# A graph layer on one core: a tile's routed rows are scattered one group later, and both adds of a pair stand together

## What is computed

```python
xn = layernorm(x)
# 1. a mean over each node's incoming edges, and a linear attention over all nodes
mean = segment_sum(xn[src], dst) / max(count, 1)
g  = relu(relu(mean @ Wl.T + bl + xn @ Wr.T) @ Wln.T + xn)
kv = einsum(k, v) / 6250              # per head, k and v normalised
m  = gelu((q @ kv + xn) @ w1 + b1) @ w2 + b2 + xn
x  = x + g + m
# 2. a mixture of experts: one shared, and for each row the best 2 of 8
xf = layernorm(x)
shared = gelu(xf @ W1s + b1s) @ W2s + b2s          # 256 -> 1024 -> 256
routed = sum over the row's 2 experts of weight * (gelu(xf @ W1p[e] + b1p[e]) @ W2p[e] + b2p[e])
out = x + shared + routed
```

## Time and profile before

| | |
|---|---|
| median of 3 runs | 3546.64 us (3541.11 to 3561.95) |
| the profiled execution | 3547.38 us, span 3545.6 us, TensorE clock 0.859 |
| TensorE, weight loads, VectorE, ScalarE, GpSimd busy | 71%, 60%, 30%, 24%, 52% |
| gathers at L508 | 1568, 995 ns each |
| scatters at L530 | 98, 1002 ns each |
| adds at L539 | 78, 1616 ns each |
| chain that ended last | TensorE 5% of the span, DMA 1% |

### The profile page before, as it was taken

One profiled execution on the slowest core, in us unless ns is written; L12 is line 12 of the kernel. 1 busy time (PEld: TensorE's weight loads), 2 busy tenths in 40 slices (PEclk: granted clock), 3 DMA queues, 4 the chain that ended last, 5 costly groups with the idle time before them and its releaser, 6 DMA issues. The chain is left out here.

```text
span 3545.6 us, 52520 instructions
## 1 busy us (share of the span) xinstructions
PE 2515.2 (71%) x12336; PEld 2115.0 (60%) x12337; DVE 1072.2 (30%) x3518; ACT 861.9 (24%) x1897; POOL 1843.6 (52%) x1790
## 2 busy tenths in 40 slices
PE   0687765655667677776868777768687787878698
PEld 0455554554556566665657666657576676666598
DVE  8344421222222223232323232223232332324221
ACT  1233211121212122221212222212122222223243
POOL 2666555545455655555455655555556556552121
PEclk9889877777779889888889898879898988989799
DMA  7333232222233343434343434343434344342564
GB/s 223 94 87 89 82 87 79 79 74 82 67 121 111 109 122 109 129 103 129 101 130 109 136 111 131 103 122 106 131 109 138 110 133 135 110 136 68 156 199 128
DMA packets 256257, 405.93 MB, mean 114 GB/s; under 512 B 70074, under 2 KB 187002, under 8 KB 255579
## 3 DMA queue, kind: packets, MB, share of 16 engines
q0 software_dynamic: 95360, 232.54, 24.2%
q1 hardware_dynamic: 154218, 164.36, 14.7%
q10 hardware_dynamic: 6384, 6.42, 0.5%
HBM read 362.16 MB, written 41.01 MB: 114 GB/s over the span
## 5 line engine op out<-in xcount | busy, mean ns | idle before, releaser
L508 POOL DMA_INDIRECT region<-xn_d,idx_s x1568 | 1560.5, 995 | 744.1 <-issue 470.8
L1380 PE MATMUL p_agg<-region,onehot 128*128 128x258 f32 x3136 | 751.5, 395 | 24.7 <-issue 15.1
L1601 PE MATMUL p_y<-region 128*128 128x256 f32 x1248 | 385.4, 444 | 438.7 <-ACT region L664 360.7
L1380 PEld LDWEIGHTS p_agg<-region,onehot 128*128 128x128 f32 x3136 | 608.4, 198 | 135.4 <-issue 43.0
L1601 PEld LDWEIGHTS p_y<-region 128*128 128x128 f32 x1248 | 270.8, 223 | 505.6 <-ACT region L664 379.3
L530 POOL DMA_INDIRECT slot_d<-xfp_s,posi_s x98 | 98.1, 1002 | 603.0 <-DVE xfp_s L1159 587.7
L664 ACT ACTIVATE region<-p_h,b_h 128x256 f32<-128x256 f32 x312 | 144.4, 473 | 921.4 <-remote 624.0
L854 DVE TENSOR_TENSOR late<-late,p_agg 128x258 f32 x176 | 74.6, 424 | 842.9 <-remote 532.8
L1590 PE MATMUL p_h<-wkv_s,region 128*128 128x256 f32 x1248 | 319.6, 384 | 9.7 <-ACT wkv_s L657 5.0
L1566 PE MATMUL p_y<-w2s_s,work 128*128 128x256 f32 x784 | 255.4, 408 | 97.5 <-ACT work L671 57.5
L848 DVE TENSOR_TENSOR onehot<-row_s,iota_s 128x896 f32<-128x896 f32 (+1 forms) x225 | 245.9, 1093 | 235.4 <-issue 232.3
(11 more groups left out here) (255 smaller groups left out, 2885.9 us busy)
## 6 DMA issues: line engine op xcount, KB each, us to landing
region<-in_w1p SPq DMA_DIRECT2D x55, 1024.0 KB
region<-in_w2p SPq DMA_DIRECT2D x55, 1024.0 KB
region<-xn_d,idx_s POOLq DMA_INDIRECT x1568
rows_s<-slot_d SPq DMA_DIRECT2D x39, 258.0 KB
region<-in_x SPq DMA_DIRECT2D x7, 896.0 KB, 5.1
xn_d<-region ACTq DMA_DIRECT2D x7, 896.0 KB, 6.5
rows<-in_x SPq DMA_DIRECT2D x49, 128.0 KB
xnr_s<-xn_d SPq DMA_DIRECT2D x49, 128.0 KB
```

What stands on the lines that cost most here:

```text
L508: pool.indirect_dma_start(out=ring[b][:, u, 0:D], out_offset=None, in_=xn_d, in_offset=IND(ap=idx_s[b][:, u:u + 1], axis=0)).then_inc(s_ro ...
L1380: m = mm(p_agg[b % 2], onehot[:, b % 2, u, :], ring[b][:, u, :], start=u == 0, stop=u == U - 1)
L1601: m = mm(p_y[:, h, :], hid2_s[:, j, h * P:(h + 1) * P], w2p_s[0][:, j, :], start=j == 0 and h == 0, stop=j == KF - 1, skip_group_check=True)
```

## The change

GpSimd's order in a step becomes: gathers of group 0, `scatter_slots`; gathers of group 1, `add_pair(0)`, `add_pair(1)`; gathers of group 2; gathers of group 3. The scatter is no longer that of the payload just being written but of the one before: a new register `paid` counts the payloads scattered (it starts at 2, the value of `pay` after the first payload), and a step scatters only if `paid` is behind `turn`. So a payload written at the end of one of TensorE's steps is scattered behind the first group's gathers of GpSimd's next iteration; an iteration without a tile does it at the same place. After the loop two scatters are left where there was one. Both adds of a pair follow the gathers of group 1. The number of DMAs of each kind is the same.

```diff
             def next_edges(edges):
                 word.look_up(edges[0] + 1)
-                plain(edges)
+                for b in range(RING):
+                    gather_edges(b)
+                    if b == 0:
+                        with pool.If_lt(paid, turn):
+                            scatter_slots()
+                pool.reg_add(turn16, turn16, 16)

             def scatter_slots():

                 pool.wait_ge(S["const"], 3)
-                pool.wait_ge(S["pay"], turn)
+                pool.wait_ge(S["pay"], paid)
                 for k in range(TOPK):
                     pool.indirect_dma_start(out=slot_d, out_offset=IND(ap=posi_s[:, k:k + 1], axis=0),
                                             in_=xfp_s[:, k, :], in_offset=None).then_inc(S["sc"], 16)
+                pool.reg_add(paid, paid, 1)
...
                 for b in range(RING):
                     if edges is not None:
                         gather_edges(b)
+                    if b == 0 and second:
+                        with pool.If_lt(paid, turn):
+                            scatter_slots()
                     if b == 1 and second:
                         with pool.If_lt(unpaired, turn):
                             pool.reg_add(pairs, pairs, 1)
                             pool.reg_add(stored, stored, 16)
-                            add_pair(0)
-                    if b == 2 and second:
-                        with pool.If_lt(one, turn):
-                            scatter_slots()
-                        with pool.If_lt(unpaired, turn):
-                            add_pair(1)
+                            for h in range(2):
+                                add_pair(h)
                             pool.reg_add(pairs32, pairs32, 32)
...
-            one = pool.alloc_register("one")
-            pool.reg_mov(one, 1)
+            paid = pool.alloc_register("paid")
+            pool.reg_mov(paid, 2)
...
             node_steps(pool, p_r, lambda it: (it, word.now() >> RING), step, next_edges)
-            scatter_slots()
+            for _ in range(2):
+                scatter_slots()
             pool.wait_ge(S["ost"], 16 * NT + 16)
```

## The result

The changed kernel took 3591.03 us (median of 4 runs, 3585.04 to 3615.49), the kernel before beside it 3554.3 (3541.11 to 3573.37): ratio 1.0134, 95% interval 1.0078 to 1.0189. It is slower by 1.3%, where 3442 us was forecast. The profiled execution took 3590.24 us for a span of 3588.4. Line 508 keeps its number; those behind the changed functions are 6 higher: L664 is now L670, L1159 is L1165.

What follows compares the result with a forecast made beforehand. No engine is full; signals crawling beside GpSimd's unbroken DMA bursts bound the kernel. 3547.4 us less 95 in the 36 pair steps and 10 in the ten before gave 3442, 8-in-10 range 3365 to 3570.

Steps and rivals of the forecast that it cites:

- The reading: All engines: after some 9 us of unbroken GpSimd DMAs, others' signals crawl until 2.4 us after the burst, setting the step.
- The scatter moved: GpSimd's burst without the payload wait starts at -2.8, ends at 17.3; others resume 5.8 us earlier, net 1.8 a step.
- The long form: Pair steps whose burst also takes in group 1's gathers: 6 expected in place of 9, each 60.0 us.
- What is late next is the work that the earlier burst cuts off: Pair's exchange between ScalarE and TensorE: two fewer hidden units get through in time, costing 4.0 us of the 5.8.
- My lower bound, -1: Worst net gain per common pair step: the cut comes still earlier and VectorE's routing falls into it, holding TensorE's count.
- Both adds behind group 1: GpSimd's later burst grows from 10.6 to 12.6 us; its gap before group 2's gathers stays except in 5 steps.
- The first ten steps: Steps before the pairs, 515.67 to 1088.09 us: earlier burst but routing cut off; 1 us gained each, 10 us.
- The slower case: Rival: the second add closes the later burst's gap, making it 21 us in 25 more steps; 3590 us, chance 0.15.
- No change: Rival: the stall follows the number of DMAs in a step, not their order; 3547 us within 18, chance 0.15.
- the hand-over: Rival: the scatter lands late, so ScalarE's copy or VectorE's payload waits for it; some 3570 us, chance 0.03.
- The Trainium skill's rule: Only VectorE and GpSimd contend, for a shared port pair; TensorE and ScalarE never wait, so gain 0: 3547 us.

Runs made afterwards that it cites:

- r3: Changed kernel with group 3's gathers held until the payload is written, where signals crawl: 3490.78 us, 0.9868 of the kernel before.
- r5: Kernel before with both adds of a pair moved behind group 1, scatter left in place, where signals crawl: 3489.7 us, ratio 0.9829.
- e7: Changed kernel with group 3's gathers held until the payload only in steps with a pair, where signals crawl: 3439.78 us, 0.9721 of the kernel before.
- r8: Changed kernel with VectorE's one-hot build cut in seven, where nothing crawls: 2663.46 us, 0.9859 of the kernel before.
- r7: Kernel before with VectorE's one-hot build cut in seven, where nothing crawls: 2664.15 us, ratio 0.9866.
- e4: Kernel before with waits between GpSimd's bursts and each add one group earlier, where nothing crawls: 2726.3 us, ratio 1.0104.
- r6: Kernel before with GpSimd's bursts broken up by waits and each add one group earlier, where signals crawl: 3315.02 us, ratio 0.9329.

## Why the prediction was wrong

**The reading held.** Signals crawl behind GpSimd's DMAs until some 2.4 us after the burst, and a pair step follows what is left at that moment. Where nothing crawls the same kernel takes 2700 us.

**The scatter moved.** Burst start -2.8 forecast, -2.6 measured; end 17.3, measured 18.0; others resume at 19.7, measured 20.5 in the step shown. Right. The long form, 9 steps to 6: it went to none, better than forecast.

**The step that failed: "What is late next is the work that the earlier burst cuts off", 4.0 us for two units.** I counted 9 us from the burst's first DMA to the cut, and moved that by 3.8 us. In the kernel before, the first 4.5 of these 9 us are two scatters and an add; signals suffer 3 to 6 us after the first *gather*, and the gathers moved from +5.5 to -2.6, by 8.1 us. Nor do the 9 us mark the onset: behind the sixth unit TensorE sums group 1, and the seventh unit's product comes only with this row of the kernel before, so ScalarE's last Gelu in time is the last before a pause:

```profile
2544.68 1.03 PE L1590 MATMUL p_h<-wkv_s,region 128*128 128x256 f32 x4
```

So 3.5 units fewer are through by the burst's end (6.1 to 2.6), and not two, and group 1's sum, between the sixth and seventh unit, slid behind the cut too. With 1.73 us for a unit (2535.79 to 2537.52 on ScalarE before) and 3.2 for the sum, that is 3.5 x 1.73 + 3.2 = 9.3 us; the burst ends 7.1 earlier in the mean. The balance is +2.2 us a step, and +2.4 was measured (61.16 - 58.78). That it fits so well is in part luck: in the table the last Gelu is 2.9 us later and the rest of the step 0.6 shorter, and the sum takes every unit at the full clock, while the lower clock adds 61 us to the `pair_up` products, 1.7 a step, of which some must lie in the exchange. How much is open. It is not the main cause: in r3 these products take 327 us, 33 more than before, and the step is 1.5 us shorter. My lower bound, -1, stopped at routing; the sum of a group was not in it. r3 confirms the step: with the start put back the same kernel gains 1.3%.

**Both adds behind group 1.** The gap before group 2's gathers stayed in 31 of 36 steps (5 forecast without it, 5 measured). Right. Apart from its 2 us in the 5.8 I took nothing for it; with the scatter left where it was, moving the adds is worth 1.7% (r5).

**The first ten steps.** 10 us forecast, 49.1 measured: what I feared there, routing cut off, did not cost. e7 carries this gain over.

**The rivals.** The slower case had the right time, 3590, and the wrong mechanism: its ungapped later burst came in 5 steps, as before, and not in 30. What it should have been is the early cut. *No change* fails: the same number of DMAs in other orders and at other times took 3315 to 4353 us where signals crawl. The wait of the hand-over (chance 0.03, 3570 us) does come where nothing crawls, 205.5 us of it on ScalarE, and costs nothing that shows (r8 against r7).

**The Trainium skill's rule.** By it the sum was 0, and the measurement says +1.3%. The crawl came in three groups of runs and not in the three others, with the same ports, so the rule neither makes nor forbids it. Where nothing crawls it does bear on the change, whose 1.0% went with the holds on GpSimd's own rows, which I had not looked for.

## What to carry to other kernels

When one event cuts another's work off, count in the timeline what is through at the new moment, unit by unit, and what stands in the queue behind the cut; a shift in time doesn't say it. Take the moment of onset from several forms of the burst before moving its head: what leads it may be harmless. Look up the clock over the busy time of the engine that works in the exchange, not over the stretch: the second can rise while the first falls. A hold that undoes only the early start, in the steps that suffer from it, kept the gain of the rest (3440 us against 3547).

## What the runs showed of the hardware

- The same kernel took 3547 to 3556 us in some groups of runs and 2700 us in others (the five groups of experiments, each on a chip of its own: 2701, 2701, 3556, 3547, 2700). That the chip makes the difference is likely and not shown. On the first sort signals of TensorE come up to 16 us late beside GpSimd's gathers; on the other GpSimd issues some 1500 DMAs unbroken with signals at 0.39 us, and a register load of SyncE takes 279 ns at most, against 702 and 708. An edit can gain 6.7% on one sort and lose 1.0% on the other (e4 and r6).
- A gather's issue on GpSimd is held by a VectorE build with both operands in SBUF that started before it, up to 0.9 us on 0.95. Cutting the 1.09 us build into seven of 0.28 us took 35 us off 2700.
- In the pair steps of the changed kernel the granted clock over TensorE's busy time was 0.895 against 0.931 in the kernel before, and a `pair_up` product took 443 against 382 ns. In the step shown the lower level came just behind 2.9 us, and within 6.0 us, in which TensorE stood still.
